# Column numbers of two one-hot comparisons moved from a PSUM bank to an f16 SBUF table, in a graph network kernel

## What is computed

```
# layer 0: msg = (x @ W)[src] * (edge_attr @ edge_w); x = ln(x + segment_sum(msg, dst) + b)
# layer 1: agg = segment_sum(x[src], dst) / max(deg, 1); x = ln(x + agg @ W_l.T + b_l + x @ W_r.T)
# layer 2: agg = segment_sum(x[src] * src_inv[src] * dst_inv[dst], dst); x = ln(x + agg @ weight + bias)
# layer 3: z = tanh(segment_sum(h[src] * norm, dst) + b); g = sigmoid(z @ gate_w + b)
#          out = relu((1 - g) * (x @ lin_w + b) + g * z); x = ln(x + batch_norm(out))
```

## Time and profile before

| | us |
|---|---|
| median of 3 runs | 3571.62 |
| profiled execution | 3552.04 |
| its span | 3550.3 |
| POOL busy / VectorE busy / TensorE busy in the span | 1616.9 / 1600.3 / 2287.1 |
| gathers L675: busy, count | 1523.0, 1612 |
| comparisons L767 and L769: busy, count | 447.2 and 348.5, 196 each |
| comparison L734: busy, count | 137.2, 202 |

### The profile page before, as it was taken

How to read it: one execution, slowest core, us unless ns; L and a number is a source line. 1 busy time by engine, 2 the same in 40 slices (tenths; PEclk the granted TensorE clock), 3 DMA queues, 4 the chain that set the end, 5 groups by cost and what they waited for, 6 DMA issues and landing times.

```text
span 3550.3 us, 35883 instructions
## 1 busy us (share of the span) xinstructions
PE 2287.1 (64%) x13014; PEld 1443.9 (41%) x13014; DVE 1600.3 (45%) x2521; ACT 498.3 (14%) x761; POOL 1616.9 (46%) x1695
## 2 busy tenths in 40 slices
PE   3365556665665566656566566566678699879970
PEld 2243334443443344334344344344444344545540
DVE  3255545555545545455545555454563411321136
ACT  0011111111111111111111111111110300201113
POOL 6665656656656655566555565555540200000000
PEclk6556666666667677777776777777789899889995
DMA  5122223323333333334343434343449677627641
GB/s 181 51 82 83 83 86 85 98 80 100 97 94 94 97 103 99 110 96 118 96 115 107 129 112 122 107 129 105 131 120 203 234 290 290 260 84 290 272 145 36
DMA packets 405652, 462.56 MB, mean 130 GB/s; under 512 B 160261, under 2 KB 298986, under 8 KB 405242
## 3 DMA queue, kind: packets, MB, share of 16 engines
q1 hardware_dynamic: 184686, 284.42, 22.9%
q0 software_dynamic: 54480, 112.65, 11.7%
q10 hardware_dynamic: 166332, 63.48, 7.3%
HBM read 372.09 MB, written 88.32 MB: 130 GB/s over the span
## 4 chain that ended last, share of the span: by engine, by line
another core or an unknown queue 38%; PE 35%; issue 9%; DVE 9%; ACT 5%; DMA 1%; POOL 1%; ACTq 1%; DVEq 1%; SPq 0%; POOLq 0%
PE pb L1384 7%; PE pb L1385 7%; PE pb L1251 5%; ACT tmp L1450 4%; PE pb L1224 4%; PE pb L1214 3%; PE pb L1172 3%; PE pb L1230 2%; PE pb L1283 2%; DVE big L769 2%; DVE big L767 1%; PE pb L1359 1%; DVE big L734 1%; PE pb L1393 1%
## 5 line engine op out<-in xcount | busy, mean ns | idle before, releaser
L675 POOL DMA_INDIRECT big<-xw,big x1612 | 1523.0, 945 | 1035.0 <-issue 534.2
L838 DVE TENSOR_TENSOR big<-pb,big 128x512 f32<-128x512 f32 x404 | 259.6, 684 | 1146.4 <-remote 835.4
L1224 PE MATMUL pb<-big 128*128 128x98 f16 x3136 | 272.0, 247 | 769.3 <-ACT tmp L1450 637.0
L1251 PEld LDWEIGHTS pb<-big 128*128 128x128 f32 x3232 | 519.4, 245 | 376.7 <-issue 368.0
L1251 PE MATMUL pb<-big 128*128 128x64 f32 x3232 | 559.1, 333 | 154.1 <-issue 139.2
L1450 ACT CAST tmp<-pb 128x784 f16<-128x784 f32 x392 | 318.3, 812 | 2116.0 <-remote 1564.1
L1224 PEld LDWEIGHTS pb<-big 128*128 128x128 f16 x3136 | 229.9, 123 | 846.3 <-issue 396.8
L1384 PE MATMUL pb<-big,yT 128*128 128x512 f16 (+1 forms) x1274 | 460.2, 369 | 31.6 <-DVE yT L1047 28.1
L1385 PE MATMUL pb<-big,yT 128*128 128x512 f16 (+1 forms) x1274 | 460.1, 369 | 0.0
L767 DVE TENSOR_TENSOR big<-pb,big 128x2048 f16<-128x2048 f32 x196 | 447.2, 2282 | 0.8
L1172 PE MATMUL pb<-big 64*128 64x512 f32 x808 | 316.6, 870 | 110.3 <-DVE big L838 82.9
(11 more groups left out here) (191 smaller groups left out, 1407.7 us busy)
## 6 DMA issues: line engine op xcount, KB each, us to landing
big<-at SPq DMA_DIRECT2D x24, 6272.0 KB, 17.9
at<-tmp SPq DMA_DIRECT2D x196, 392.0 KB
big<-at ACTq DMA_DIRECT2D x32, 896.0 KB
big<-xw,big POOLq DMA_INDIRECT x1612
big<-in_ea SPq DMA_DIRECT2D x202, 64.0 KB
big<-at SPq DMA_DIRECT2D x13, 896.0 KB
big<-at ACTq DMA_DIRECT2D x24, 336.0 KB
tmp<-at ACTq DMA_DIRECT2D x8, 896.0 KB
```

The source lines that it names most:

```text
L675: nc.gpsimd.indirect_dma_start(gath[:, T8 * (n % NG) + t % T8, :], None, xw_d, bass.IndirectOffsetOnAxis(ap=src_i[:, t:t + 1], axis=0)).th ...
L838: nc.vector.tensor_tensor(msg[:, T8 * (n % 2) + 4 * q:T8 * (n % 2) + 4 * q + 4, :], PB[:, q, :].rearrange("p (t f) -> p t f", f=D), gath[: ...
L1224: last = nc.tensor.matmul(PB[:, 4 + g, i * KW:i * KW + KW], hot_lo[:, at_pair, :], hot_key[:, at_pair, :], start=True, stop=True)
L1251: last = nc.tensor.matmul(PB[:, 2 + n % 2, 0:WIN], msg[:, T8 * (n % 2) + t, :], hot_win[:, T8 * (n % 2) + t, :], start=(t == 0), stop=(t = ...
```

## The change

`cols` becomes an SBUF tensor of 226 f16 values in each partition, filled by the same two copies L728 and L729. L767 and L769 read it there, so that both of their inputs and their result are f16 in SBUF. `window_hot` (L734) reads the f32 row `cols_pf` in SBUF in place of the bank. In step 5 fifteen short instructions on one partition raise the entries of `win_tab` from step STEP_OF[g] on to at least the first row that is still open, and `window_add` of step 14 waits once for `s_off`.

```diff
+        cols = sb("cols", [P, P + KW], F16)
-        cols = PB[:, 7, 0:P + KW]
             def window_hot(n):
-                nc.vector.tensor_tensor(hot_win[...], cols[:, 0:WIN].unsqueeze(1).broadcast_to([P, T8, WIN]),
+                nc.vector.tensor_tensor(hot_win[...], cols_pf[:, 0:WIN].unsqueeze(1).broadcast_to([P, T8, WIN]),
             def window_add(n):
+                if n == STEP_OF[0]:
+                    v.wait_ge(s_off, 1)
                 win_at = v.value_load(win_tab[0:1, n:n + 1], min_val=0, max_val=NP)
                 if n == 5:
                     for g in range(NG1):
-                        last = nc.vector.tensor_scalar(flags[:, 3 + g:4 + g], half_i[...], float(GB * P * (g + 1)), None, ALU.is_lt)
+                        nc.vector.tensor_scalar(flags[:, 3 + g:4 + g], half_i[...], float(GB * P * (g + 1)), None, ALU.is_lt)
+                        here = win_tab[0:1, STEP_OF[g]:STEP_OF[g + 1] if g + 1 < NG1 else NH]
+                        last = nc.vector.tensor_scalar(here, here, float(GB * P * (g + 1)), None, ALU.max)
                     last.then_inc(s_off, 1)
```

More of the change, by code:

```diff
@@ L733, in window_hot @@
                 at_tile = T8 * (n % 2)
-                nc.vector.tensor_tensor(hot_win[:, at_tile:at_tile + T8, :], cols[:, 0:WIN].unsqueeze(1).broadcast_to([P, T8, WIN]),
+                nc.vector.tensor_tensor(hot_win[:, at_tile:at_tile + T8, :], cols_pf[:, 0:WIN].unsqueeze(1).broadcast_to([P, T8, WIN]),
                                         rel[:, n * T8:n * T8 + T8].unsqueeze(2).broadcast_to([P, T8, WIN]), ALU.is_equal).then_inc(s_hotw, 1)
@@ L852, in _ @@
                     for g in range(NG1):
-                        last = nc.vector.tensor_scalar(flags[:, 3 + g:4 + g], half_i[:, STEP_OF[g]:STEP_OF[g] + 1], float(GB * P * (g + 1)), None, ALU.is_lt)
+                        nc.vector.tensor_scalar(flags[:, 3 + g:4 + g], half_i[:, STEP_OF[g]:STEP_OF[g] + 1], float(GB * P * (g + 1)), None, ALU.is_lt)
+                        here = win_tab[0:1, STEP_OF[g]:STEP_OF[g + 1] if g + 1 < NG1 else NH]
+                        last = nc.vector.tensor_scalar(here, here, float(GB * P * (g + 1)), None, ALU.max)
                     last.then_inc(s_off, 1)
```

## The result

The changed kernel took 3379.41 us (median, 3377.77 to 3389.88) beside 3572.22 us for the kernel before: a ratio of 0.9476, 95% interval 0.9457 to 0.9495. It is 5.2% faster. I had forecast 3890 us, 8.9% slower. The profiled execution took 3377.77 us, its span is 3376.0 us.

What follows compares the result with a forecast made beforehand. It took POOL's gather stream, about 3 us to VectorE's release and 2.1 us to POOL's restart as the bound. Median 3571.6 + 322 us of held gathers = 3893.6, given as 3890 us; range 3640 to 3960 us.

Steps and rivals of the forecast that it cites:

- The comparisons' duration: L767 and L769 on VectorE: two bytes gain nothing, times stay 2282 and 1778 ns.
- The lock on the gathers: Gathers started inside L767 or L769 end about 0.81 us after them: 1.64 us a step, 322 us in all.
- s near 1: s is how many us into L767 a gather starts; near 1 in long steps, first delay 2.15 - s.
- the pairs: Loop steps alternate one long, one short: 24.8 us for two, with 16 gathers in a row.
- the middle: Gather delay per step at the middle of the range 1.2 to 2.45 us: 1.83 us.
- no turn: Rival: POOL gets no turn between L767 and L769, so the first gather waits for both: 603 us, 4175 us; chance 0.06.
- The transmission: In the loop, all 322 us of gather delay lies between two POOL pauses and reaches the loop's end.
- Faster: Rival: 1.6 us pauses at delayed gathers bring the late release sooner; 445 us gained against 322 lost, about 3450 us; chance 0.06.
- Swallowed: Rival: POOL's 500.8 us of waiting for L838 takes up the 322 us: 3572 us, no change; chance 0.08.
- double rate: Rival: two bytes halve L767 and L769 to 1.21 and 0.95 us; gathers held 79 us, 3650 us; chance 0.10.
- the sign that I had named for it: If gathers lengthen and POOL's wait for L838 shortens by as much, the delay was absorbed by that wait.
- The small parts: Fifteen new instructions in step 5 take 1 to 2 us more, hidden behind POOL's gathers; step 14's wait is already over: nothing.

Runs made afterwards that it cites:

- e3: The changed kernel with its SBUF table in f32 in place of f16: 3381.28 us, ratio 0.951 to the kernel before.
- e7: The kernel before with POOL at most two groups ahead of VectorE: 2990.9 us, ratio 0.9998, in a session where the kernel before took 2991.43 us.
- e5: The kernel before with POOL pausing for two small fills after each group's second gather, from step 4: 3121.96 us, ratio 1.0438 (kernel before 2991.43 us).
- e8: The kernel before with POOL pausing for five small fills after each group's second gather, from step 0: 3347.88 us, ratio 1.1195 (kernel before 2991.43 us).
- e1: The kernel before with only L767 and L769 reading an f16 table in SBUF: 3380.25 us, ratio 0.9486.
- e6: The kernel before with one short POOL fill after each of the eight gathers, from step 4: 3291.44 us, ratio 1.1002 (kernel before 2991.43 us).

## Why the prediction was wrong, step by step

**The comparisons' duration: right.** 2284 and 1781 ns with all operands in two bytes, forecast unchanged from 2282 and 1778. What the Trainium skill (Vector Engine (DVE) Microarchitecture Reference, section 5.1) measured, that one element read again and again as a 2-byte input of a two-source instruction runs at one a cycle, agrees with these rows, and e3 puts f32 beside it: 2287 ns.

**The lock on the gathers (VectorE holding a gather until 0.81 us after its own end): right, and its sum a little small.** Of some 420 gathers of over 1.15 us in the changed kernel, 388 end within 0.06 us of 0.81 us after the end of L767 or L769. The mean of L675 was forecast at 1145 ns and is 1176, 372 us in place of 322, 1.90 us a step in place of 1.64. The mis-sized term is the start of the first gather: I laid the delays over the positions of before, where each long step starts with s near 1; without the pairs s is spread out, and the middle that I had worked out without them, 1.83, is the better figure. The gathers spared for starting just ahead are also fewer than I had read from the rows: in the changed kernel two that start 0.08 and 0.10 us into L767 are held, where I had put the limit at 0.13. POOL got its turn between L767 and L769, so "no turn" fell. The Trainium skill (SBUF — State Buffer, Who interferes with whom) says that a VectorE instruction with two SBUF inputs contends with a GpSimd instruction that reads SBUF, and these rows agree, a gather's row numbers being in SBUF; its inference that tensor_tensor leaves descriptor generation alone is contradicted by them.

**The transmission: wrong, and this is the step that failed.** I wrote that the period is 16 gathers, then about 3 us, then 2.1 us, that POOL's 500.8 us "is the tail of each period, which starts when POOL is done", and that what delays POOL delays the pair. The observation was right: the release follows the end of POOL's stream. I took the order of events for a chain of work, in which the gathers bring something that VectorE needs. The runs show that they bring nothing for this release. In each nameless wait of steps 5 to 197 of the kernel before, VectorE's own last gather had been issued 34 us and more before; where VectorE does wait for its gather, in e7, it starts 1.5 to 5.5 us after the issue. What it lacked was TensorE's signal, which came late beside POOL's unbroken stream. A chain gets longer with its links; a delay that a stream causes gets shorter when the stream has holes. So the term I had added, 322 us at the end of the loop, was really there as 372 us, and the wait of 500.8 us that I had called the tail of each period, to stay as it is, fell to 17.6. It could have been read from the trace of the kernel before. Its step 2, TensorE and then VectorE:

```profile
84.62 3.67 PE L1251 MATMUL pb<-big 128*128 128x64 f32 x16
```

```profile
125.36 1.29 DVE L838 TENSOR_TENSOR big<-pb,big 128x512 f32<-128x512 f32 x2 [42.08 <-remote]
```

TensorE was done with the window at 88.29, 37 us before VectorE starts, and the last gather of that step had ended at 86.6. The wait is on TensorE's semaphore: the trace has the count of `s_pe` at 125.34, 0.02 us before L838. I had compared the ends of POOL's and VectorE's rows only, and not asked how long TensorE had been done. The page of the kernel before warned of it too, in the chain that ended last:

```profile
another core or an unknown queue 38%; PE 35%; issue 9%; DVE 9%; ACT 5%; DMA 1%; POOL 1%; ACTq 1%; DVEq 1%; SPq 0%; POOLq 0%
```

POOL, from which I had the whole period follow, has 1% of it, and what has no name 38%. In the changed kernel it is 52% and 4%.

**The rival that came true.** "Faster: each delayed gather is also a pause" had the mechanism, at a chance of 0.06 and 3450 us. I argued against it with the pause of 5.12 us at each pair's start. That pause does work, as in the rows above: the signals come through in it. But then 20 us of unbroken stream follow. A pause once in two steps isn't a pause in each step. The price was too small as well: I freed half of the pairs at the full cost to POOL, and the loop lost nearly all that the late signals cost. In the comparison at the top that is 3572.2 - 2991.4 = 581 us (the prompt time taken from e5 to e8), and less 372 us of longer gathers it gives 209 us, for 193 measured; the rest is what still comes late.

**Swallowed and double rate: fell.** By the sign that I had named for it, a wait for L838 that shrinks by as much as the gathers grow, the delay would count as swallowed: the wait shrank by 483 us, the gathers grew by 372. But a swallowed delay leaves 3572 us. The wait shrank because VectorE is no longer late, so the sign didn't tell the two apart.

**The small parts: right.** L853 of before is L855 and L857 of after; with the fifteen new instructions they take from 154.97 to 157.01, 2.04 us in place of 0.99 and 0.24 of idling. VectorE is late by 0.9 us with the messages of step 6, and POOL streams on beside it. e1, which has neither the clamps nor the window comparison, has the time of the changed kernel.

**What I couldn't have read.** That the same kernel takes 2991 us in other sessions. There POOL bounds the loop from the start, and by the nearly one-for-one rows of e5, e6 and e8 the change would cost its 372 us: about 3363 us, 12% slower, an estimate. The prediction's sum would then hold, but for its 322 in place of 372, from 2991 us. This wasn't run: four runs of the changed kernel all fell into late sessions.

## What to carry to other kernels

When an engine is released at a fixed time after another has run dry, ask first whether the second produces anything that the first needs; if not, it isn't a chain, and slowing it may free the first. For each nameless wait look up how long its true producer has been done. And a gain that comes from slowing an engine down is a gain against a disturbance: here 1.8 us of idling a step gives 5.9% where TensorE's signals are late and costs 12% where they are not, while holding POOL two groups ahead gives 0.6% (0.3 to 0.9) in the one and nothing in the other, the only one of the versions run in both that is slower in neither.

## What the runs showed of the hardware

- Beside a stream of indirect DMAs from POOL, one each 1.25 us, without a hole, TensorE's signals to ScalarE, VectorE and SyncE came 3 to 37 us late in some sessions (the kernel before). In the kernel before 46 of VectorE's 65 late starts came 2.4 to 3.4 us after POOL's last gather, the latest 7.6 us after it (step 2); 58 of ScalarE's 153 came in the middle of the stream. In other sessions the same stream, nearly unbroken for 2000 us, delayed none of the 392 to ScalarE by over 2.6 us.
- In the same sessions TensorE's 16 products of a window spread over up to 13 us; in the prompt ones they took 3.68 us at most.
- No signal of VectorE or ScalarE was late in the trace of the kernel before: TensorE starts 0.06 us after the message that it waits for and 0.15 us after the copy, POOL 0.8 or 2.4 us after the message.
- What makes a session late is open, and so is which part of POOL's stream does the harm. A run with half the bytes came into a prompt session. Instruction loading isn't it in the two long stalls (88 to 125 us of the kernel before, 2401 to 2429 us of the changed one): none of its packets lie in them.
- The time lost falls with the sum of POOL's pauses per step, not from a length on: 570, 396, 137 and 6 us lost at 0, 0.66, 1.5 and 1.8 us. The number of late signals does not fall before 1.8; the long delays do.
- Where both inputs of a VectorE comparison are in SBUF, an indirect DMA that POOL starts inside it ends 0.81 us after it (388 of some 420 in the changed kernel); with one input in PSUM, in the kernel before, they take 945 ns on average.
